# Decoder block on one core: Gram parts split between ScalarE and VectorE, statistics merged, first-group steps reordered

## What is computed

```python
# attention, per sequence and head (chunks of 32 tokens)
q, k, v = silu(conv4(x @ Wq)), silu(conv4(x @ Wk)), silu(conv4(x @ Wv))
q, k = l2norm(q), l2norm(k); kb = k * beta; v = v * beta
inv = -(kb @ k.T) * strict_lower      # then 31 steps of forward substitution
u = inv @ v; w = inv @ kb             # then a scan over the 4 chunks
attn = (q @ k.T) * lower_incl
# four sources (short filter, long filter, delta rule, v), of each head:
stats = mean, var, mean |.|, l2       # 16 numbers per token
p = softmax(gelu([x, stats] @ Wg1) @ Wg2 / temp)      # mixes the four sources
o = rmsnorm(mix * sigmoid(gelu([x, stats2] @ Wog1) @ Wog2)) @ Wo
# experts
top_vals, top_idx = top_k(softmax(x @ Wg), 2)         # ties: the lower index first
```

## Time and profile before

| | |
|---|---|
| median of 3 timed runs | 478.71 us (477.77 to 479.16) |
| the profiled execution | 474.98 us, of which the span is 473.3 us |
| TensorE matrix products, busy | 379.8 us, 80% |
| VectorE busy | 316.1 us, 67% |
| ScalarE busy | 152.4 us, 32% |
| GpSimd busy | 41.1 us, 9% |
| mean granted clock | 0.870 |

### The profile page before, as it was taken

The page is one execution under the profiler, slowest core; times in us unless marked ns, Lnnn a source line. Parts: engine busy times, 40 slices in busy tenths (PEclk is TensorE's granted clock), DMA queues, the critical chain, the costliest instruction groups (busy, mean ns, idle before and its releaser), DMA issues.

```text
span 473.3 us, 8308 instructions
## 1 busy us (share of the span) xinstructions
PE 379.8 (80%) x2952; PEld 273.6 (58%) x2952; DVE 316.1 (67%) x1045; ACT 152.4 (32%) x260; POOL 41.1 (9%) x116
## 2 busy tenths in 40 slices
PE   0979997778689999737566699987989889988992
PEld 0546664557578986726434366655566655664762
DVE  1142673998979581884984767768877588777635
ACT  1223342138222243314220153322452233414340
POOL 6000001830830000000000000000000000000000
PEclk9989999799955665959777599998999889999998
DMA  7560202098934000001010000000200000000000
GB/s 243 136 192 8 46 0 68 1 250 232 233 67 91 3 2 1 1 1 39 7 46 0 22 2 0 24 0 2 67 0 24 0 0 22 0 1 0 25 1 23
DMA packets 48580, 22.25 MB, mean 47 GB/s; under 512 B 17785, under 2 KB 47649, under 8 KB 48545
## 3 DMA queue, kind: packets, MB, share of 16 engines
q1 hardware_dynamic: 32032, 13.40, 11.1%
q10 hardware_dynamic: 16512, 8.39, 6.3%
HBM read 18.64 MB, written 3.15 MB: 46 GB/s over the span
## 4 chain that ended last, share of the span: by engine, by line
PE 54%; DVE 30%; DMA 6%; issue 4%; ACT 3%; SPq 1%; ACTq 0%; DVEq 0%
PE bank L755 10%; PE bank L763 10%; PE bank L498 7%; PE bank L480 4%; PE bank L780 3%; DVE as_t L1343 3%; DVE inv L1355 3%; DVE prod L1353 3%; PE bank L795 2%; DMA inverses<-inv 2%; DMA cb<-cbundle 2%; PE bank L806 2%; PE bank L656 1%; DVE as_t L1395 1%; DVE wtap L1440 1%
## 5 line engine op out<-in xcount | busy, mean ns | idle before, releaser
L763 PEld LDWEIGHTS bank<-w_sb,as_t 128*128 128x128 f32 x512 | 60.9, 193 | 22.5 <-issue 16.7
L763 PE MATMUL bank<-w_sb,as_t 128*128 128x128 f32 x512 | 63.8, 280 | 5.0 <-ACT as_t L1085 5.0
L1085 ACT ACTIVATE as_t<-bank,cb 128x512 f32<-128x512 f32 x64 | 43.3, 687 | 74.5 <-PE bank L755 59.2
L755 PE MATMUL bank<-as_t,w_sb 128*128 128x512 f32 x128 | 64.6, 631 | 0.0
L498 PE MATMUL bank<-wtap,xc_pad 128*128 128x384 f32 x128 | 47.0, 514 | 6.1 <-DVE wtap L1299 6.1
L1590 DVE SCALAR_TENSOR_TENSOR as_t<-bank,as_t 128x128 f32<-128x128 f32 x128 | 36.0, 343 | 23.7 <-PE bank L763 21.3
L498 PEld LDWEIGHTS bank<-wtap,xc_pad 128*128 128x128 f32 x128 | 24.6, 201 | 23.3 <-DVE wtap L1299 6.5
L755 PEld LDWEIGHTS bank<-as_t,w_sb 128*128 128x128 f32 x128 | 23.6, 204 | 19.3 <-issue 17.9
L480 PE MATMUL bank<-ident,as_t 128*128 128x128 f32 (+1 forms) x64 | 12.1, 319 | 26.9 <-DVE as_t L1510 10.7
L1343 DVE TENSOR_TENSOR as_t<-bank,masks 128x512 f32 (+1 forms) x32 | 20.0, 689 | 13.5 <-PE bank L532 13.4
L780 PE MATMUL bank<-vb,early 32*32 32x32 f32 x512 | 25.6, 222 | 3.5 <-DVE vb L1604 1.9
(11 more groups left out here) (232 smaller groups left out, 617.7 us busy)
## 6 DMA issues: line engine op xcount, KB each, us to landing
toep<-taps_long ACTq DMA_DIRECT2D x8, 1024.0 KB, 8.3
toep<-x SPq DMA_DIRECT2D x8, 256.0 KB, 2.9
early<-x SPq DMA_DIRECT2D x4, 256.0 KB, 4.9
w_sb<-w SPq DMA_DIRECT2D x1, 1024.0 KB
w_sb<-w SPq DMA_DIRECT2D x2, 512.0 KB
blocks<-as_t SPq DMA_DIRECT2D x16, 64.0 KB, 3.2
early<-blocks SPq DMA_DIRECT2D x2, 512.0 KB, 4.0
inverses<-inv SPq DMA_DIRECT2D x2, 512.0 KB, 5.3
```

The lines of the kernel that those rows point to most:

```text
L755: pe.matmul(ps[4 + half][:, :], w1_sb[:, e, half * 128:half * 128 + 128], x2_c.rearrange("p b t -> p (b t)"), start=True, stop=True).then_ ...
L763: last = pe.matmul(bank(6 + e % 2)[:, b, :], hid[:, e % 2, half, b * L:(b + 1) * L], w2_sb[:, e, half, :], start=(half == 0), stop=(half = ...
L1085: act.activation(hid[:, e % 2, half, :], ps[4 + half][:, :], ACT.Relu, bias=c_of("b1", 2 * e + half)).then_inc(s["hid_ready"], 1)
```

## The change

It does five things.

1. The upper half of each Gram bank (256 of the 512 columns) is copied by ScalarE without a mask (`keep_upper`); what the mask made zero is not read. VectorE masks the other 256 columns, after ScalarE's copy from the same bank. `blocks_to_dram` waits for both.
2. The order of VectorE's work around the inverse: all six first columns of half 0 come after `norms(3)` and the masks of group 2; the other cuts move too.
3. `source_moments` can take two groups. Groups 2 and 3 are done in one call behind `step(1)`, with 128 columns each instruction. That of group 1 goes behind `source_sums(7)`, sums 9 and 10 behind `rotate_keys(0)`.
4. `choose` makes one table of differences and one comparison instead of two comparisons and two products, and sums 256 columns, not 512. Five GpSimd constants become three.
5. On TensorE `short_filter(3)` goes ahead of `st2_transposed(0)`, `output_gate(0)` ahead of `outputs(3)`, `values(0)` ahead of `wo(0)`; ScalarE follows.

```diff
@@ blocks_to_dram
                 sp.wait_ge(s["gram_kept"], 2 * H * (g + 1) + credit["gram_kept"])
+                sp.wait_ge(s["upper_kept"], 2 * H * (g + 1))
@@ gpsimd: masks and tie
-            pool.memset(masks[:, :, :], 1.0).then_inc(pool_step, 1)
-            pool.memset(tie[:, :, :, :], 1.0).then_inc(pool_step, 1)
+            pool.memset(mask[:, :], 1.0).then_inc(pool_step, 1)
+            pool.memset(tie[:, :, :], 0.0).then_inc(pool_step, 1)
...
@@ tensor
             v_transposed(3)
+            short_filter(3)
             st2_transposed(0)
             outputs(2)
+            output_gate(0)
             outputs(3)
-            output_gate(0)
-            short_filter(3)
             output_z(0)
...
             ont(0)
+            values(0)
             wo(0)
-            values(0)
             keys(0)
@@ scalar
+            def keep_upper(g, r):
+
+                rows_of = as_t[:, :, 0, :].rearrange("p (b h) t -> p b h t", h=H)
+                for h in range(H):
+                    act.wait_ge(s["gram_ps"], g * 2 * H + r * H + h + 1 + credit["gram_ps"])
+                    act.activation(rows_of[:, bass.ds(g * G + 2 * r, 2), h, :], bank(4 + h, 2)[:, :, 0:L], ACT.Copy
+                                   ).then_inc(s["upper_kept"], 1)
+
             def project_step(g, more):
                 activate(g, 0)
                 keep_keys(g - 1)
-                for b in range(1, G):
-                    activate(g, b)
+                activate(g, 1)
+                activate(g, 2)
+                keep_upper(g - 1, 0)
+                activate(g, 3)
                 square_qk(g)
                 if more:
                     xc_columns(g + 1)
                 gate_tanh(g)
+                keep_upper(g - 1, 1)
                 keep_q_v(g)
...
             keep_keys(NG - 1)
+            keep_upper(NG - 1, 0)
             keep_long(0)
             keep_long(1)
+            keep_upper(NG - 1, 1)
...
             v_columns_kept(3)
+            keep_short(3)
+            squares(8)
             st2_columns(0)
             keep_outputs(2)
+            output_gate(0)
             keep_outputs(3)
-            output_gate(0)
-            squares(8)
-            keep_short(3)
+            output_tanh(0)
             squares(9)
-            output_tanh(0)
-            squares(10)
-            squares(11)
             ctx_columns(0)
             on_columns(0)
             keep_values(0)
+            squares(10)
+            squares(11)
@@ vector: mask_products
-                rows_of = as_t[:, :, :, :].rearrange("p (b h) k t -> p b h (k t)", h=H)
+                rows_of = as_t[:, :, 1, :].rearrange("p (b h) t -> p b h t", h=H)
                 for h in range(H):
-                    dve.wait_ge(s["gram_ps"], g * 2 * H + r * H + h + 1 + credit["gram_ps"])
-                    dve.tensor_tensor(out=rows_of[:, bass.ds(g * G + 2 * r, 2), h, :], in0=bank(4 + h, 2),
-                                      in1=mid(masks[:, :, :].rearrange("p k t -> p (k t)"), 2),
-                                      op=ALU.mult).then_inc(s["gram_kept"], 1)
+                    dve.wait_ge(s["upper_kept"], g * 2 * H + r * H + h + 1)
+                    dve.tensor_tensor(out=rows_of[:, bass.ds(g * G + 2 * r, 2), h, :], in0=bank(4 + h, 2)[:, :, L:],
+                                      in1=mid(mask[:, :], 2), op=ALU.mult).then_inc(s["gram_kept"], 1)
@@ vector: order around the inverse
-            solve_columns(0, 0, 6)
             mask_products(NG - 2, 0)
             gate_sums(NG - 1)
             norms(NG - 1)
             mask_products(NG - 2, 1)
-            solve_columns(0, 6, 9)
+            solve_columns(0, 0, 6)
             mask_products(NG - 1, 0)
-            solve_columns(0, 9, 11)
+            solve_columns(0, 6, 8)
             mask_products(NG - 1, 1)
-            solve_columns(0, 11, CH - 1)
+            solve_columns(0, 8, CH - 1)
...
-            solve_columns(1, 0, 20)
+            solve_columns(1, 0, 22)
             subtract_applied(1, 0)
-            solve_columns(1, 20, 24)
+            solve_columns(1, 22, 26)
             subtract_applied(1, 1)
-            solve_columns(1, 24, CH - 1)
+            solve_columns(1, 26, CH - 1)
@@ vector: source_moments
-            def source_moments(g):
+            def source_moments(first, groups=1):
...
-                dve.sem_inc(s["stats_ready"], 1)
+                dve.sem_inc(s["stats_ready"], groups)
@@ vector: choose
-                for k, op in enumerate((ALU.is_ge, ALU.is_gt)):
-                    own(dve.tensor_tensor(out=cmp_[:, :, :, k, :], in0=score.unsqueeze(2).broadcast_to([128, G, E, E]),
-                                          in1=wide(score, E), op=op))
-                for k in range(2):
-                    own(dve.tensor_tensor(out=cmp_[:, :, :, k, :], in0=cmp_[:, :, :, k, :],
-                                          in1=tie[:, k, :, :].unsqueeze(1).broadcast_to([128, G, E, E]), op=ALU.mult))
+                own(dve.tensor_tensor(out=cmp_, in0=score.unsqueeze(2).broadcast_to([128, G, E, E]),
+                                      in1=wide(score, E), op=ALU.subtract))
+                own(dve.tensor_tensor(out=cmp_, in0=cmp_, in1=tie[:, :, :].unsqueeze(1).broadcast_to([128, G, E, E]),
+                                      op=ALU.is_gt))
@@ vector: group 0
             mixture(0)
-            source_moments(1)
             source_sums(6)
             dve.wait_ge(pool_step, 14)
             mixture_stats(0)
             source_sums(7)
+            source_moments(1)
             source_sums(8)
             gated(0)
             scale_delta(2)
             scale_delta(3)
-            source_sums(9)
-            source_sums(10)
             dve.wait_ge(w_late, 16 * LATE_LOADS)
             x1_norm(0)
             rotate_keys(0)
-            source_moments(2)
+            source_sums(9)
+            source_sums(10)
             source_sums(11)
-            source_moments(3)
...
             step(1, False)
+            source_moments(2, 2)
```

52 lines of the change are left out of this document (24 added, 28 removed).

## The result

| | before | after |
|---|---|---|
| median (lowest to highest) | 478.24 us (475.35 to 479.16, 4 runs) | 464.80 us (462.18 to 464.85, 4 runs) |
| profiled execution, time | 474.98 us | 464.75 us |
| its span | 473.3 us | 463.0 us |

The ratio is 0.9715, with a 95% interval of 0.9661 to 0.9770: 13.4 us less where 10.3 were forecast, and 464.8 us where 468.4 were. Both spans differ by exactly 10.3 us.

A forecast was written before the change was run, and what follows sets the result against it. The prediction took TensorE (54% of the chain) and VectorE (30%) to bound the kernel by turns. Its terms, 5.3 + 10.8 + 1.5 - 7.3 = 10.3 us less, took 478.7 to 468.4 us, range 461.5 to 474.

The forecast's parts named there:

- Part 1: Gram bank masks: four half masks take 1.45 us, four ScalarE copies 1.2 us, and each half pass saves 1.03 us.
- Part 2: VectorE's order around the inverse: half 0 solved at 113.9, not 118.05, 4.1 us earlier; 5.3 us won by 155 us.
- Toeplitz load: The last Toeplitz load, which competes with the inverse's transfer, was to come 6.6 us earlier.
- Parts 3 and 5: Group 0's statistics and gate order: 7.9 + 6.3 - 3.4 = 10.8 us won at rotate_queries(0) (9 to 12.7).
- the 3.4: New VectorE idle time ahead of x1_norm(0), which waits for wo(0): about 3.4 us, 1.5 with the clock high.
- The clock: TensorE's clock at the groups' scores: 3 us won if it stays up, 0 if it falls; middle value 1.5 us.
- The late pass: Merged moments of groups 2 and 3 behind step(1): TensorE pauses 5.5 us, then low clock; 7.3 us lost (5.0 to 9).
- Rival (a): Merged moments pass behind step(1) is cheap, so the 7.3 us loss vanishes: 461.1 us; chance 0.12.
- Part 4, the ranking: choose in every step: about 1.1 us of VectorE work saved four times, but 0 won since TensorE is waited for.
- (b): Half 0's inverse is bound by transfers or the filter and arrives as before; 5.3 us don't come: 473.7 us; chance 0.12.
- (c): Inverse's 5.3 us missing, group 0 gives 9, clock nothing, late pass costs 9: 478.7 us, no measurable change; chance 0.06.
- (d): ScalarE becomes the bound of the projection loop; at 1.2 us a copy the kernel is slower, 483.8 us; chance 0.08.

The follow-up runs named there:

- columns_first: Changed kernel with half 0's first six inverse columns back ahead of the masks of group 2, ScalarE copies kept; 464.12 us, ratio 0.9732.
- masks_whole: Changed kernel with VectorE masking all 512 columns again and no ScalarE copies of the upper halves; 469.43 us, ratio 0.9817.
- pass_later: Changed kernel with the moments pass over groups 2 and 3 moved from behind step(1) to ahead of start_sum(1) within it; 456.76 us, ratio 0.9574.
- choose_two: Changed kernel with the old ranking, two comparisons and two tables instead of one difference table and one sum; 466.20 us, ratio 0.9765.
- all_three: Changed kernel with the late pass ahead of start_sum(1), source_sums(9) ahead of x1_norm(0), and half 0's columns in old order; 451.18 us, ratio 0.9454.
- pass_within: Changed kernel with the moments pass over groups 2 and 3 moved from behind step(1) to ahead of x2_norm(1) within it; 459.39 us, ratio 0.9645.
- gate_order_old: Changed kernel with TensorE's and ScalarE's old order around group 0's output gate, VectorE's new order kept; 464.90 us, ratio 0.9777.
- the repeat: The changed kernel run once more, with no edit; 463.94 us, ratio 0.9743.

## Why the prediction was right, and where it was not

**Part 1.** Right. Four half masks 1.42 us (1.45 worked out), four copies 1.21 (1.2). Undone alone it costs 3.6 us at the inverse. The Trainium skill, "ScalarE: Activation LUTs", section "Rules for kernel authors", says that adds and multiplies belong on VectorE, which it gives as up to about 3x faster in bf16. Taken over to these float32 copies, as an estimate, that ratio would have made the four 3.6 us; the trace has 1.21, so it doesn't carry over to them.

**Part 2.** Total right, split wrong. Half 0 was solved at 114.09 (forecast 113.9, 4.1 us earlier; measured 3.96), and 5.43 us were won at the solution (forecast 5.3). But part 1 alone gives 5.16 us at the transfer and 6.3 at the solution (154.69 to 148.35), and the new order on top of it takes 1.2 back at the transfer. The step that failed is the gain from "`norms(3)` starts there, not at 87.11". It starts there (81.44), but the sum held the blocks' return at before's 80.31 us. In columns_first, with the half masks, it is at 77.70, and of the 4.2 us of the six columns half lies in VectorE's idle time. I costed the second edit against the kernel before, not against the kernel with the first edit in it. Even against the kernel before it was put too high: the order's share of the 4.1 us was about 1 us, and masks_whole shows 0.40, because the six columns in their new place take 5.0 us (90.40 to 95.42) and not 4.2.

The Toeplitz load that was to come 6.6 us earlier came 2.6 earlier (114.73, 117.35). With a median of 7.4 us from issue to landing it still ran beside the inverse's transfers, where the four issues now took 6.22 us.

**Parts 3 and 5.** Right at `rotate_queries(0)`: VectorE had no idle time ahead of `gated(0)`, 2.91 us ahead of `x1_norm(0)` (forecast 3.4), and TensorE's scores came 16.15 us earlier, 5.3 + 10.8 = 16.1 forecast. There is a slip in the 3.4: 5.5 us less 1.3 are 4.2, and with 4.2 the sum would have been 9.5 us. The runs split the 10.7 that were measured behind the solution: about 3.9 us hang on TensorE's and ScalarE's order and about 4.9 on VectorE's, each less what its inverse was late. They aren't independent, and 1.9 us are in neither.

**The clock.** Wrong: of the middle value of 1.5 us nothing came. It fell at the first scores after 1.99 us of idle time. That it can stay up after 2.12 us is seen in pass_later, and is worth 3.4 us there, so both ends of that term, 0 and 3, were seen; the middle was neither.

**The late pass.** Right in mechanism and size. Step 1 grew from 58.56 to 65.87 us, 7.3 us, as forecast; the pause was 5.22 us (5.5), the first of the `queries` behind it ran at the lower level (1.92 us, forecast 1.91). The slope that the pass was costed with is 258 / 256 = 1.01 ns a column, not 1.03, which changes nothing in the sum; the pass took 4.8 us where 5.0 were forecast. pass_later puts the price at 7.6. Rival (a) was rightly held unlikely for this place, and its 7 us could be had by another place.

**Part 4, the ranking.** Wrong. "0" should have been about 1 us in each full step that has the clock up (1.09 us in step 2, a wait of 0.79 in step 3 of choose_two), and 0 where the clock is down. I looked for VectorE's lead at the scores' transposition; the instruction that waits is `st2_transposed`, for `start_sum`. In before this was covered by a lower clock.

**The sum.** The last 1.45 us of the span's 10.3 came in step 2, where the clock term had been meant to come: before's step took 56.04 us with the clock down in part, after's 54.59 with it up. With the clock up the old ranking still leaves 55.68 us (choose_two), so 0.36 us is the clock's alone and 1.09 needed the new ranking as well. Step 3 gave nothing, since the clock was down for a part in both (57.45 and 57.44 us). So 10.3 was met by 8.84 from the first three terms (5.3 + 10.8 - 7.3 = 8.8) and 1.45 from one that I had not in the sum. The forecast of 468.4 missed the measured 464.8 because I kept the distance of 3.7 us between before's profile and its median for the change too; later medians of before were 476.47, 476.92, 476.69 and 475.27 us, so 478.7 was on the high side, and after's profile lay on its median. The timed gains of 12.75 and 13.4 us are still 2.5 to 3 us above the forecast's 10.3. One later step moves as much with the clock; whether that is the cause, the runs don't show.

**The rivals.** (b) and (c) fell: the inverse went out at 114.09 us, its last issue ended 4.4 us earlier than in before (123.75, 128.17), and the solution came 5.43 us earlier. In part (b) has a point, since of the 1.2 us that columns_first and all_three win at the transfer 0.1 us may be all that arrives. (d) fell with copies of 0.30 us.

## What to carry to other kernels

Cost a second edit against the kernel that has the first in it: two edits that end the same wait don't add (5.16 and 0.40 us alone, 3.96 together), and one may then cost. Work that must be done before a certain point belongs into an idle stretch of its own engine that lies behind the critical step and ahead of its reader; the same 4.8 us pass cost 7.6 us, 3.5 us or nothing by its line in the program alone. Where the clock moves whole steps by 3 us, compare profiles from mark to mark at equal clocks, ask at which mark a difference arises before you give it to the edit, and a wait that isn't in the trace of before may only be hidden by a low clock there.

## What the runs showed of the hardware

TensorE's clock was not settled by the instruction stream alone. The same step 3 took 54.39 us with the clock up and 57.44 with a mean of 0.58 in one stretch of 4 us, in two executions of one program. At the first scores it fell in 1.99 us and 2.06 us of idle time (scores at 235.12 and 234.75 us) and held in 2.09, 2.12 and 2.27 us (pass_within, pass_later, gate_order_old). In the stretch of 32x32 products it stood at 0.50 from 140 to 155 us in all fourteen profiles, while TensorE was busy for 4.0 us or more of every 5. It rose for a part of 155 to 165 us in after and for a part of 160 to 170 us in before; only masks_whole's profile lacks this rise.

The four transfers that bring half 0's inverse back took 6.22 us to be issued in after (from 117.53), 3.25 in the repeat (from 119.96), 6.88 in all_three (from 116.59), and 2.28 in masks_whole (from 125.39). In the twelve kernels with half masks the first issue began between 116.59 and 120.54 us, and the last ended between 123.12 and 124.54: something that these edits don't move seems to hold SyncE's queue there. ScalarE's queue had issued its last 1 MB Toeplitz load between 113.70 and 116.26 us in these kernels. Whether that load holds the other queue I didn't try. Transfers hold 2% of after's chain.
